# Three expert tiles of known tokens placed between the steps of the last two attention blocks

## The reference

```python
# attention: per step t and head
s = s * w_ + (s @ a_) b_ + v_ k_        # state update
y = s @ q_                              # then group norm, gate, Wo
x = _layernorm(x + attention(x))
# experts: E = 8, D = 256, F = 1024
assign = argmax(x @ centroids.T)        # one expert for each of 4096 tokens
xn = layernorm(x) * ln_g[e] + ln_b[e]
h  = relu(xn @ W1[e] + b1[e])
y  = x + h @ W2[e] + b2[e]
x  = _layernorm(x + y)
```

## Time and profile before

| | before |
|---|---|
| median of 3 runs | 1100.58 us |
| profiled execution, its own time | 1097.72 us |
| its span, first to last instruction | 1095.6 us |
| PE busy | 1022.3 us (93%) |
| DVE busy | 791.7 us (72%) |
| POOL busy | 680.4 us (62%) |
| ACT busy | 541.2 us (49%) |
| mean granted TensorE clock | 0.972 of 2.4 GHz |

### The profile page before, as it was taken

The page is one execution under the profiler, slowest core; times in us unless marked ns, Lnnn a source line. Parts: engine busy times, 40 slices in busy tenths (PEclk is TensorE's granted clock), DMA queues, the critical chain, the costliest instruction groups (busy, mean ns, idle before and its releaser), DMA issues.

```text
span 1095.6 us, 42592 instructions
## 1 busy us (share of the span) xinstructions
PE 1022.3 (93%) x16832; PEld 840.8 (77%) x16833; DVE 791.7 (72%) x1777; ACT 541.2 (49%) x1113; POOL 680.4 (62%) x1135
## 2 busy tenths in 40 slices
PE   8998999999999999998999999589899999999995
PEld 5676777787777777776877777567799988889894
DVE  4776888887887788887878877237466666666663
ACT  4475676676685676675766857122122212222220
POOL 1088888888888978987979878830223333323321
PEclk9999999999999999999999999679999999999998
DMA  4113224234134133142252341828454545545430
GB/s 104 40 20 80 70 40 101 59 54 108 32 81 105 23 92 92 30 98 60 53 106 44 71 99 23 249 64 286 179 181 150 179 161 170 178 150 179 148 126 5
DMA packets 208625, 112.04 MB, mean 102 GB/s; under 512 B 172364, under 2 KB 191952, under 8 KB 208080
## 3 DMA queue, kind: packets, MB, share of 16 engines
q1 hardware_dynamic: 202080, 100.77, 34.0%
q0 software_dynamic: 3744, 8.40, 2.2%
q10 hardware_dynamic: 2640, 0.54, 0.2%
HBM read 85.42 MB, written 26.08 MB: 102 GB/s over the span
## 4 chain that ended last, share of the span: by engine, by line
PE 58%; POOL 18%; DVE 8%; DMA 7%; issue 6%; ACT 1%; SPq 1%; DVEq 0%; POOLq 0%; ACTq 0%
PE bank L953 12%; PE bank L561 11%; POOL arena L1897 9%; PE bank L966 9%; POOL arena L1900 8%; PE bank L699 4%; PE bank L646 4%; PE ry L966 4%; PE bank L654 3%; PE bank L607 2%; DMA arena<-scr_n 2%; DMA scr_n<-arena 2%; DMA arena<-scr_u 2%; DMA scr_u<-arena 1%; DVE arena L1485 1%
## 5 line engine op out<-in xcount | busy, mean ns | idle before, releaser
L1900 POOL TENSOR_TENSOR arena<-arena 128x30 f32<-128x30 f32 (+14 forms) x480 | 296.0, 617 | 37.6
L1897 POOL TENSOR_TENSOR arena<-arena 128x30 f32<-128x30 f32 (+14 forms) x480 | 283.7, 591 | 36.4
L561 PE MATMUL bank<-arena 128*128 128x256 f32 (+2 forms) x992 | 266.1, 406 | 4.4 <-DVE arena L1403 2.7
L561 PEld LDWEIGHTS bank<-arena 128*128 128x128 f32 x992 | 175.1, 196 | 47.5 <-issue 21.0
L953 PEld LDWEIGHTS bank<-arena 128*128 128x128 f32 x1248 | 146.8, 194 | 5.5 <-issue 2.7
L953 PE MATMUL bank<-arena 128*128 128x128 f32 x1248 | 147.3, 277 | 3.2 <-DVE arena L1806 2.5
L1485 DVE TENSOR_TENSOR arena<-bank,arena 128x512 f32<-128x512 f32 x128 | 79.5, 683 | 32.4 <-PE bank L646 32.3
L1296 ACT ACTIVATE arena<-arena 128x1 f32<-128x1 f32 x39 | 11.5, 295 | 176.6 <-DVE arena L1760 176.6
L1931 POOL COPY arena<-arena 128x1 int32 (+1 forms) x39 | 7.1, 181 | 146.6 <-DVE arena L1824 146.6
L966 PE MATMUL bank<-arena 128*128 x416 | 96.4, 385 | 0.1
L966 PEld LDWEIGHTS bank<-arena 128*128 128x128 f32 x416 | 76.9, 190 | 14.5 <-issue 4.9
(11 more groups left out here) (174 smaller groups left out, 1792.0 us busy)
## 6 DMA issues: line engine op xcount, KB each, us to landing
arena<-in_W SPq DMA_DIRECT2D x47, 1024.0 KB, 5.0
scr_n<-arena SPq DMA_DIRECT2D x64, 128.0 KB, 2.9
arena<-scr_n SPq DMA_DIRECT2D x16, 512.0 KB, 3.7
scr_u<-arena SPq DMA_DIRECT2D x16, 512.0 KB, 3.0
arena<-scr_u SPq DMA_DIRECT2D x62, 128.0 KB, 2.8
arena<-in_xTp SPq DMA_DIRECT2D x32, 132.0 KB, 4.0
arena<-in_x SPq DMA_DIRECT2D x64, 64.0 KB, 2.0
scr_x<-arena SPq DMA_DIRECT2D x64, 64.0 KB, 2.5
```

The lines of the kernel that those rows point to most:

```text
L561: mm = pe.matmul(ring.tile(m, name)[0:rows, to], lhsT, rhs, start=(i == 0), stop=(i == len(terms) - 1))
L1897: inv_ok.inc(f"m{s}", TT(t, U[:, 0:s, s:s + 1].broadcast_to(shape), U[:, s:s + 1, s + 1:TB].broadcast_to(shape), ALU.mult))
L1900: inv_ok.inc(f"a{s}", TT(U[:, 0:s, s + 1:TB], U[:, 0:s, s + 1:TB], t, ALU.add))
```

## The change

KNOWN falls from 28 token tiles to 24 (blocks 0 to 11), and all of their placing moves from bodies 16 and 17 into body 15. A new `early_blocks` finds, among the full groups of 128 known tokens of each expert, the first three (EARLY) as tiles 0 to 2. A new `rank_early` on PE and `early_rows` on DVE make their part of `table`. POOL gathers the three tiles in body 16; their two layers stand between the steps of bodies 16, 17, 18 and of the routing, in place of `keep_busy`. The remaining 36 tiles run behind, as before. SP loads the rows `ln_g`, `ln_b`, `b2` and the first W1 in bodies 15 and 16, where it had loaded them behind the attention. The scratch x1 is stored step-major, so that known tokens are its first rows, and `rows_of_out` turns its row numbers into those of the output. Because four more token tiles are late, the chain of carries `c0` to `c3` becomes `c0` to `c7`.

```diff
-KNOWN = NTILE - 2 * NTILE_BLK
+KNOWN = NTILE - 4 * NTILE_BLK
+EARLY = DEPTH
...
-        x1d = nc.dram_tensor("scr_x1", (B, T, C), F32, kind="Internal").ap()
+        x1d = nc.dram_tensor("scr_x1", (T, B, C), F32, kind="Internal").ap()
...
+            def first_early_weights():
+                chain_pe.wait(sp, last - 1, "Y")
+                ring.wait_full(sp, last - 1, "su")
+                load_row(0)
+                sp.wait_ge(soon.sem, soon.value(0, "expert"))
+                load_w1(0, 0)
+            def more_early_weights():
+                load_w1(1, 1)
+                load_row(2)
+                load_experts(slice(4, E))
+                load_w1(2, 2)
+                for e in range(E):
+                    sp.wait_ge(w2_in[e], 16)
+                    sp.sem_inc(w2_ready, 1)
...
+            def turn_early(j):
+                chain_act.wait(pe, last, "ye", "yo")
+                prep.wait(pe, j, "l")
...
+            def first_early(j, half_of):
+                xnT_ok.wait(pe, j, "x")
+                pe.wait_ge(w1_in[j], 16)
...
                 if n == last + 2:
-                    keep_busy(2, idle_ps)
+                    turn_early(1)
+                    first_early(1, 0)
...
                     project_out(n - 2)
                 if n == last + 2:
-                    keep_busy(7, idle_ps)
-                if n == last + 1:
+                    first_early(1, 1)
+                    second_early(0, 0)
+                if n == last:
                     rank_known()
...
+                if n == last:
+                    rank_early()
                 if has(n - 1):
                     centre_y(n - 1)
                 if n == last + 1:
-                    keep_busy(3, idle_ps)
+                    turn_early(0)
+                    first_early(0, 0)
...
# DVE, body
+                if n == last:
+                    place_known()
+                    early_blocks()
                 if has(n - 1):
                     keep_x_odd(n - 1, 1)
...
                     keep_x_odd(n - 1, 0)
+                if n == last:
+                    mark_slots(0, KNOWN // GROUP)
+                if n == last + 1:
+                    prepare_stats(0, 0)
...
# DVE, behind the bodies
+            relu(1, 1)
+            early_row(2)
+            keep_xnT(2)
             late_act.wait(dve, last, "lg")
             one_hot(route, slice(KNOWN, NTILE))
+            prepare_z(2, 2)
+            finish_stats(0, 0)
...
+            early_end(0)
+            relu(2, 2)
+            finish_stats(1, 1)
+            early_end(1)
             dve.wait_ge(route_pe.sem, route_pe.value(0, "table"))
...
# POOL
             for s in range(DEPTH):
                 gather(s, s)
+            scatter(0, 0)
+            scatter(1, 1)
+            pool.wait_ge(table_ok, 1)
+            pool.wait_ge(x1_out, NBLK * 64)
+            for s in range(DEPTH):
+                gather(EARLY + s, s)
```

More of the change, by code:

```diff
@@ L32 @@
 NTILE = NTOK // P
+EMPTY = 2 * NTOK - 1
 EBLK = NTILE + E - 1
@@ L777, in rank_known, with turn_x @@
                 route_pe.inc("known", pe.matmul(rank_ps[:, KNOWN * E:2 * KNOWN * E], all_ones, oh, start=True, stop=True))
+            def turn_x(j, s):
+                prep.wait(pe, j, "l")
+                if not (isinstance(j, int) and j == 0):
+                    xnT_ok.wait(pe, j - 1, "x")
+                for k in range(HALF):
+                    mm = pe.transpose(xnT_ps[:, k * P:(k + 1) * P], xn[:, k * P:(k + 1) * P], ident)
+                turned_x.inc("x", mm)
+            rounds, ahead = {}, [0]
@@ L800, in body @@
                     keep_busy(1, ring.tile(n - 3, "logit"))
+                if n == last + 3:
+                    second_early(0, 1)
+                    turn_early(2)
                 if has(n - 3):
@@ new lines, in _ @@
+            R("nblk")
+            route.inc("left", TT(left, blocks, taken, ALU.subtract))
+            R("left")
+            route.inc("bend", nc.vector.tensor_tensor_scan(blk_end, ones[:, 0:E], left, float(EARLY), ALU.mult, ALU.add))
+            R("bend")
+            route.inc("bstart", TT(blocks, blk_end, blocks, ALU.subtract))
+            places(route, slice(KNOWN, NTILE))
+            R("bstart")
+            route.inc("first", TT(place, blocks[:, None, :].broadcast_to([P, NTILE, E]), onehot, ALU.mult))
@@ new lines, in _ @@
+            R("first")
+            route.inc("of", red(posf, place, AX.X, ALU.add))
+            R("of")
+            R("relf")
+            route.inc("blkf", TT(blkf, posf, relf, ALU.add))
+            R("blkf")
+            for g in range(2):
+                some = slice(g * (NTILE // 2), (g + 1) * (NTILE // 2))
+                wide = [P, NTILE // 2, EBLK]
+                route.inc(f"here{g}", TT(here[:, some], cst["eblock"][:, None, :].broadcast_to(wide),
+                                         blkf[:, some, None].broadcast_to(wide), ALU.is_equal))
+                R(f"here{g}")
+                for w, name in enumerate(("high", "low")):
+                    route.inc(f"{name}{g}", TT(in_blk[:, some, w], here[:, some], cst[name][:, some, None].broadcast_to(wide), ALU.mult))
@@ L1846, in iteration @@
                 known = isinstance(j, int)
-                before, after = not (known and j == 0), lambda n: not (known and j + n >= EBLK)
+                before, after = not (known and j == EARLY), lambda n: not (known and j + n >= EBLK)
                 if before:
```

635 lines of the change are left out of this document (389 added, 246 removed).

## The result

| | before | after |
|---|---|---|
| median | 1100.58 us (5 runs, 1098.72 to 1102.94) | 1113.84 us (5 runs, 1109.9 to 1118.78) |
| profiled execution, its span | 1097.72, 1095.6 us | 1113.84, 1111.5 us |
| mean granted TensorE clock | 0.972 | 0.956 |

The ratio is 1.0133, with a 95% interval of 1.0102 to 1.0164: slower by 1.3%, about 14.6 us. I had forecast slower by 4.5 us, and the time lies above my range (1113.0). A second comparison gave 1.0149 (1.0112 to 1.0187).

A forecast was written before the change was run, and what follows sets the result against it. PE bounds the tile loop; behind solve(15) one dependent chain over PE, ACT and DVE does. -22.9 (tiles) + 21.1 (chain) + 3.3 (solve(15)) + 3.0 (clock) = +4.5 us on 1100.58: 1105.1 us, range 1096.5 to 1113.

The forecast's parts named there:

- Tiles removed: In the full-PE loop, three of 39 tiles at 7.65 us each go, none of it hidden: -22.9 us.
- Solve(15), +3.3: Body 15: POOL's inverse 4.3 us longer beside new DVE work, SP's loads 0.2, less 1.2 us of slack.
- if POOL is later: Body 15: PE's 0 to 2 us lost to DVE's placing do not decide, as POOL's inverse comes 4.3 us later.
- Items 1 to 5 and the clock: Solve(15) to one-hot: inserted tile steps lengthen the chain, and PE's waits lose 3.0 us of clock; 15.7 us together.
- item 1: Centring to variance of block 15: tile 0's statistics and first half layer stand ahead, +4.3 us.
- items 2 and 3: Variance to output projection: tile 0's other half layer +0.9; its relu, then tile 1's half layer queued ahead +3.8 us.
- items 4 and 5: Projection to one-hot: tile 2's statistics and half a second layer +0.8; router(15) queued behind tile 2's transpose +2.9 us.
- Items 6 to 9: One-hot to first gather: DVE steps +1.4, more carries +1.7, tile ends before the table +4.2, POOL's scatter first +1.1 us.
- item 8: DVE between `expert` and `table`: two tile ends, a relu, `finish_stats` and ACT's root delay the gather, +4.2 us.
- high end: Upper limit of the forecast: solve(15) at 8.5 and clock 6, +12.7 us, 1113 us.
- bounds of solve(15): Limits on how far solve(15) moves: 0.3 and 8.5 us, around the 3.3 taken.
- The rival that is faster: Items 1 to 6 overlap 7 us more than counted, so the tiles fit in: -4.1 us, 1096.5 us; chance 0.25.

The follow-up runs named there:

- experiment 2: Kernel before with a fifth x1 store per block: 1.0033; as control, kernel before with x1 stored block by block, stores in the old form: 0.9996.
- the fifth store's kernel: Kernel before with one more store of x1 per block, of the same form, to a scratch of its own: 1.0033, 3.6 us.
- experiment 7: Changed kernel with table and gathers ahead of tile ends and scatters: 1.0106; also with tile 2's own PSUM bank, earlier relu, fewer idle matmuls: 1.0076.

## Why the prediction was wrong

The direction was right, and the size was 9 us short.

- **Tiles removed, -22.9 us:** as predicted.
- **The step that failed is one that the sum does not have.** I worked out bodies 15 to 18 and the routing, and put the store of x1, which changed in each of 16 blocks, at nothing without a reason. The step-major store alone is +0.85%, 9.4 us, and nothing once it stands behind the inverse. Its issue went from 0.43 to 0.595 us on SP's queue; how much of the 9.4 us is that is open (experiment 2). The diff shows the line, and the prediction does not mention it.
- **Solve(15), +3.3: the size was about right, the path was wrong.** Memset to solve(15) rose by 5.2 us in the changed kernel's trace (46.18 to 51.40). Over the profiles it is 50.2 on average for eleven with the change (46.4 to 53.6) and 46.6 for five without: +3.7, or +2.9 with the fifth store's kernel, which had 51.2. POOL's inverse took 37.9 to 38.2 us in the eleven kernels and 35.0 to 35.1 in six with the old body 15, so +3.0 where I had 4.3. But PE did not wait for it. Of DVE's placing I had said that PE loses 0 to 2 us by it and that this does not decide "if POOL is later". In the changed kernel's trace it did: DVE made its copies of block 14's results behind the placing, PE stood 1.85 us for them and then ran into solve(15) without a wait. In ten of the eleven traces it is so, with waits of 1.6 to 2.9 us for DVE; the eleventh waited 1.04 us for the inverse. From solve(14) to solve(15) it is 39.6 us instead of 35.6, 4.0 of the 5.2. Beside the 1.85 us, steps of PE ahead of solve(15) ran at half clock, such as this one, which had taken 1.99 us:

```profile
739.49 3.60 PE L600 MATMUL bank<-arena 128*128 128x8 f32 x12
```

  DVE's copies, and the queues of SP and ACT ahead of solve(15):

```profile
716.66 1.27 DVE L1629 COPY arena<-bank 64x512 f32<-64x512 f32 x2
```

```profile
728.72 0.35 SPq L540 DMA_DIRECT2D arena<-in_ln_g  x1
730.14 0.42 SPq L537 DMA_DIRECT2D arena<-in_W  x1
731.40 2.94 SPq L474 DMA_DIRECT2D scr_x<-arena  x4
734.88 0.36 SPq L497 DMA_DIRECT2D scr_u<-arena  x1
739.12 2.73 SPq L466 DMA_DIRECT2D arena<-in_x  x4
741.95 1.14 SPq L508 DMA_DIRECT2D arena<-scr_u  x2
```

```profile
741.31 1.02 ACTq L1306 DMA_DIRECT2D arena<-scr_u  x2
```

  The inverse was close behind all the same. Its loads were issued at 741.31 and 741.95, 7.1 us behind POOL's end on SP (4.4 us before). `load_tokens` (L466), which waits for the landing of x1, stands ahead of SP's half alone, and ACT's half was 0.6 us earlier, so most of that is the landing of the store of the inverse, 5.4 us (4.4 before), with two loads of 1 MB begun ahead of it; that these slow it was not tried. Loads of this kind took some 3 us to land, so I estimate that PE would have waited for them had it come 2 us earlier.
- **Items 1 to 5 and the clock, 15.7:** 15.5 measured. Within it the parts are off: variance moved by 7.0 us (16.14 from solve(15), 9.13 before) where item 1 has 4.3, for its half layer ran at half clock; variance to projection by 6.9 (13.06 against 6.19) where items 2 and 3 have 4.7; projection to one-hot by 1.6 (9.58 against 7.95) where items 4 and 5 have 3.7. Running PE's steps in the other order gave 5.3 us back in the trace, so the waits in order are shown.
- **Items 6 to 9, 8.4:** 8.7 measured as the gather's delay. But item 8 called these steps ones that "keep the gather waiting though nobody waits for them". They do: without them the gather came 5.5 us earlier. But experiment 7 shows that tile 3's first layer did not come earlier with it, because of tile 2's second layer and the idle matmuls. The size was right; that the gather decides was wrong.
- **Not priced:** 1.3 us between gather and first layer.

Together -22.9 + 3.7 + 15.5 + 8.7 + 1.3 = +6.3 us. Without the store's cost the changed kernel measured 1.0073 and 1.0066, 8.0 and 7.3 us. With 9.4 us for the store the sum is 15.7, against 14.6 and 16.4 us measured. My high end had room for POOL and the clock, and none for a part that I had not looked at.

**Slips in my sums.** The high end leaves the chain at 21.1 us, though its own bound was 23; with that it is +14.6 us, 1115.2 us, and would have held the measured 1113.84 us, by luck, since no term stands for the store. The bounds of solve(15), 0.3 and 8.5, are not the sums of their terms, which give 0 and 10.5. Block 14's inverse lasted 40.0 us (648.52 to 688.55), not 39.6. The rate of 188 GB/s in the earlier trace rows makes 5.6 us of 1 MB, not 3. The rival that is faster speaks of 1 us for the clock and adds 1.5. None of these moves the forecast by more than 0.3 us.

## What to carry to other kernels

Price each edit in a loop's body before those at its edge: another form of four stores in each of 16 blocks outweighed the placing of three tiles, and moving the stores behind the work that others wait for took the cost away. A change of layout is a change of DMA form, so read the issue time of that queue in the trace and what stands behind it. When two paths end within 2 us of each other, check in the new trace which one was waited for: here the forecast had the right size by the wrong path. When a step is said to hold up a chain, ask what else the next step waits for; idle matmuls that hold the clock are themselves work in PE's order.

## What the runs showed of the hardware

- The issue of a 64 KB store on SP's queue took 0.43 us as 32 x 2 x 256, with 32 rows side by side in DRAM, and 0.595 us as 64 x 1 x 256 with rows 4 KB apart: equal bytes, as many rows of 1 KB.
- Six back-to-back DVE instructions with both inputs in SBUF held one POOL instruction for 4.40 us in one kernel, and took turns with it in another. POOL's inverse keeps its length within 0.4 us over eleven kernels (37.9 to 38.2 us), while memset to solve(15) around it scatters by 7 us.
- A wait of PE of 1.0 to 1.7 us ahead of solve(15) was followed by half clock: solve(15) took 5.02 and 6.40 us instead of 3.92, and the stretch behind it 4 and 6 us more than in kernels of the same steps without the wait.
- The time of one program varies between executions by 10 us and more. One profile cannot carry a difference of that size. The length of a single stretch often can, unless the clock differs in it.
